# Zeroing the experts' row table ahead, in the first attention, instead of padding behind each expert's last row

## The reference, cut to what matters

```
L0 attention: h = silu(x W1' + b1) W2' + b2;  q,k,v = h Wg' + bg  (16 heads of 64)
              dots = q k' / 8, masked where j >= i + 64; softmax; @ v; @ Wo' + bo
L0 ffn:       logits = -|x - keys|^2 + x rw' + rb  over 16 experts; the best 4; w = softmax(top 4)
              expert e: gelu(x w1[e]' + b1[e]) w2[e]' + b2[e]  (512 hidden);  sum of the 4 by w
L1 attention: 16 heads of 8, LoRA of rank 16 on all four projections
L1 ffn:       a scan of gates over 16 steps of 256 rows, then tanh
```

## Time and profile before

| | |
|---|---|
| median of 3 runs | 1598.92 us (1596.56 to 1600.42) |
| the profiled execution's own time | 1603.28 us |
| its span, first to last instruction | 1601.5 us |
| mean granted TensorE clock | 0.921 of full |
| first attention | 0 to about 691 us |
| first transpose of the experts | 712.1 us |
| HBM read / written | 46.87 / 27.33 MB |

### The profile page before, as it was taken

How to read it: one execution, slowest core, us unless ns; L and a number is a source line. 1 busy time by engine, 2 the same in 40 slices (tenths; PEclk the granted TensorE clock), 3 DMA queues, 4 the chain that set the end, 5 groups by cost and what they waited for, 6 DMA issues and landing times.

```text
span 1601.5 us, 37212 instructions
## 1 busy us (share of the span) xinstructions
PE 1305.1 (81%) x9486; PEld 975.0 (61%) x9486; DVE 1059.0 (66%) x3801; ACT 960.6 (60%) x2716; POOL 785.4 (49%) x898
## 2 busy tenths in 40 slices
PE   7999999999999999746799999703778777787871
PEld 3766666666666666436799999602445445455540
DVE  1677777777777777637766666414776767777646
ACT  5877777777777777423455555302565656556654
POOL 1567777777777777624400000276656655652003
PEclk9999999999999999958999999956898989889986
DMA  9100000000000000021122222123423223232101
GB/s 343 45 8 16 13 11 13 13 13 13 13 13 13 13 13 14 16 66 55 49 66 66 66 66 66 54 50 54 81 49 77 54 51 75 46 72 43 31 0 53
DMA packets 77063, 75.02 MB, mean 47 GB/s; under 512 B 10913, under 2 KB 66977, under 8 KB 75330
## 3 DMA queue, kind: packets, MB, share of 16 engines
q1 hardware_dynamic: 67506, 56.86, 13.9%
q0 software_dynamic: 8192, 16.79, 3.8%
q10 hardware_dynamic: 1296, 0.59, 0.1%
HBM read 46.87 MB, written 27.33 MB: 46 GB/s over the span
## 4 chain that ended last, share of the span: by engine, by line
PE 32%; issue 6%; ACT 5%; DVE 5%; POOL 3%; DVEq 2%; POOLq 2%; SPq 1%; DMA 0%; ACTq 0%
PE psum L818 8%; PE psum L829 7%; PE psum L862 3%; PE psum L851 3%; PE psum L926 3%; POOL yk L567 2%; ACT qst L1098 2%; PE psum L942 2%; PE psum L943 1%; ACT wall L1054 1%; ACT wall L1098 1%; DVE wA L1292 1%; PE psum L798 1%; PE psum L884 1%; DVEq L1431 1%
## 5 line engine op out<-in xcount | busy, mean ns | idle before, releaser
L503 POOL TENSOR_SCALAR P<-P,rinv 128x192 f32<-128x192 f32 (+1 forms) x384 | 308.8, 818 | 164.4 <-DVE rinv L1170 162.7
L1010 ACT ACTIVATE P<-shifted,least 128x192 f32<-128x192 f32 (+1 forms) x512 | 240.2, 471 | 126.4 <-DVE least L1156 125.1
L1044 ACT ACTIVATE hid<-psum,wA 128x128 f32<-128x128 f32 x576 | 164.9, 369 | 146.8 <-PE psum L818 146.7
L1368 DVE TENSOR_REDUCE mx<-psum 128x2 f32<-128x512 f32 x256 | 164.4, 685 | 82.6 <-PE psum L926 79.2
L1156 DVE CUSTOM_DVE_ANT_0 shifted<-psum,band 128x192 f32<-128x192 f32 (+1 forms) x512 | 168.7, 384 | 30.5 <-PE psum L695 30.2
L1054 ACT ACTIVATE wall<-psum 128x1024 f32<-128x1024 f32 x128 | 131.2, 1025 | 83.5 <-PE psum L851 81.2
L818 PE MATMUL psum<-xgT,wA 128*128 128x128 f32 x1152 | 162.3, 285 | 18.0 <-DVE xgT L1299 16.3
L818 PEld LDWEIGHTS psum<-xgT,wA 128*128 128x128 f32 x1152 | 143.7, 196 | 25.6 <-issue 25.3
L493 POOL DMA_INDIRECT xs<-x1c,pos x128 | 128.0, 1000 | 55.9 <-issue 28.2
L829 PE MATMUL psum<-wB,hid 128*128 128x128 f32 x1152 | 154.0, 278 | 0.0
L567 POOL DMA_INDIRECT yk<-ys,posc x128 | 123.7, 967 | 49.5 <-issue 37.1
(11 more groups left out here) (247 smaller groups left out, 2671.8 us busy)
## 6 DMA issues: line engine op xcount, KB each, us to landing
xg<-xs SPq DMA_DIRECT2D x144, 64.0 KB, 1.8
ys<-yrow SPq DMA_DIRECT2D x72, 128.0 KB, 1.9
wall<-in_wall SPq DMA_DIRECT2D x1, 8232.0 KB, 36.6
qkd<-parts SPq DMA_DIRECT2D x32, 192.0 KB
qst<-qkd SPq DMA_DIRECT2D x66, 64.0 KB
wall<-qkd SPq DMA_DIRECT2D x35, 64.0 KB
kst<-qkd SPq DMA_DIRECT2D x11, 192.0 KB
hT<-in_xT SPq DMA_DIRECT2D x4, 512.0 KB, 6.1
```

The lines of the kernel that those rows point to most:

```text
L503: g.tensor_scalar(x, x, rinv[:, par, n:n + 1], None, ALU.mult).then_inc(s["pn_ready"], 1)
L1010: last = sc.activation(P[:, par, it, h, 0:w], shifted[:, par, it, h, 0:w], ACT.Exp, scale=-1.0, bias=least[:, par, n:n + 1], accum_out=row ...
L1044: sc.activation(hid[:, p, f, :], UP[two][:, at:at + GT], ACT.Gelu, bias=wA[:, p, F + f:F + f + 1]).then_inc(s["hid_ready"], 1)
L1368: v.tensor_reduce(out=mx[:, :, h], in_=SB[(par + 1 + h) % 3].rearrange("q (i n) -> q i n", i=TT), axis=mybir.AxisListType.X, op=ALU.max).t ...
```

## The change

The fill no longer depends on the counts. SyncE, once it has issued the weight loads, writes zeros over the whole table in 34 transfers: 33 of them write 128 rows of each of the 16 sections (1 MB, in pieces of 512 bytes), the last writes the 128 rows at `DUMMY` (64 KB). From the fifth on, two are let go a batch, by `wo_mm`. An even one also waits until the earlier ones have landed. GpSimd gets one more wait a batch, ahead of the first scatter: the rows that this batch can reach must be filled. All pads, their `value_load`s, three VectorE instructions (L1269 to L1271) and ScalarE's two waits go.

```
-        def pad(eng, e):
-            at = eng.value_load(pad_at[0:1, e:e + 1], min_val=0, max_val=DUMMY) if e < E else DUMMY
-            eng.dma_start(xs[bass.ds(at, GT), :], zrow[:, :]).then_inc(s["pad_in"], 16)
...
+            sp.wait_ge(s["zrow_ready"], 1)
+            rows = xs[0:DUMMY, :].rearrange("(e r) d -> r e d", e=E)
+            nothing = zrow[:, :].rearrange("q (o d) -> q o d", o=1).to_broadcast([128, E, D])
+            for c in range(CAP // 128):
+                if c % 2 == 0 and c > 0:
+                    sp.wait_ge(s["filled"], 16 * c)
+                if c >= 4:
+                    sp.wait_ge(s["wo_mm"], PAIRS * (c // 2 - 1))
+                sp.dma_start(rows[128 * c:128 * c + 128, :, :], nothing).then_inc(s["filled"], 16)
+            sp.dma_start(xs[DUMMY:ROWS, :], zrow[:, :]).then_inc(s["filled"], 16)
+
             sp.wait_ge(s["plan_ready"], 1)
             sp.dma_start(plan_d, plan2[:, :, :].rearrange("q k c -> q (k c)")).then_inc(s["plan_out"], 16)
-            sp.wait_ge(s["zrow_ready"], 1)
-            for e in range(3):
-                pad(sp, e)
             sp.wait_ge(s["plan_out"], 16)
             sp.dma_start(plan[:, :], plan_d.rearrange("(o t) c -> o (t c)", o=1)).then_inc(s["plan_in"], 16)
-            for e in range(3, E // 2):
-                pad(sp, e)
             sp.wait_ge(s["plan_in"], 16)
-            sp.wait_ge(s["pad_in"], 16 * (E + 1))
+            sp.wait_ge(s["filled"], 16 * (CAP // 128 + 1))
...
                         if p == 0:
                             need_alone(pool, "pos_ready", b - 1)
+                            need_alone(pool, "filled", 32 * (b - 1))
...
-            act.wait_ge(s["plan_ready"], 1)
-            act.wait_ge(s["zrow_ready"], 1)
-            for e in range(E // 2, E + 1):
-                pad(act, e)
...
-            v.tensor_tensor(skip[:, :], count[:, :], first_row[:, :], ALU.add)
-            v.drain()
-            v.tensor_copy(pad_at[:, :], skip[:, :])
```

More of the change, by code:

```diff
@@ L128, in build @@
         past = sb("past", [128, E])
-        skip = sb("skip", [128, E])
         ended = sb("ended", [128, 2, E])
@@ L135, in build @@
         plan2 = sb("plan2", [128, 2, 2], i32)
-        pad_at = sb("pad_at", [128, E], i32)
         plan = sb("plan", [1, 512], i32)
@@ L277, in build @@
             m_y var_ready pow_ready x1c_ready m_x x1T_ready m_l mask_ready m_r pos_ready xsq_ready x1_kept scat exp_w top_ready
-            ksq_ready rmat_ready a_done plan_ready zrow_ready plan_out plan_in pad_in
+            ksq_ready rmat_ready a_done plan_ready zrow_ready plan_out plan_in filled
             b2_mm xg_in0 xg_in1 xg_in2 xg_in3 tin_mm xgT_ready wA_ready wB_ready up_mm hid_ready dn_mm yrow_ready ys_out
```

## The result

The changed kernel is faster: 1589.93 us against 1600.29 (medians of 11 runs each), ratio 0.9948 with an interval of 0.9936 to 0.9961, about 8 us (the two medians by themselves lie 10.4 apart). Forecast were 2.3 us, 1596.6, and 1594 to 1603.

What follows compares the result with a forecast made beforehand. TensorE sets the pace, waiting at the experts' start on SyncE's pads. Removing them gives -2.4, GpSimd's wait +0.15, faster scatters -0.05, fills nothing: -2.3 us, 1598.92 to 1596.6; own range 1594.5 to 1598.5, overall 1594 to 1603.

Steps and rivals of the forecast that it cites:

- the three VectorE instructions: Plan ahead of the experts: with the drain, about 0.4 us earlier, but the plan isn't last; worth nothing.
- What bounds the kernel: TensorE sets the pace; between attention and experts it idles 15.09 us behind SyncE's queue of `value_load`s and pads.
- So the 2.4 us go through to the end.: Expert stage: one pipeline of row loads, weight copies and products, so an start 2.4 us earlier shortens the whole kernel.
- Fills: First attention: 34 fills, 34.7 MB at 287 GB/s, two in about 9 us with start and landing; cost nothing.
- rival 1: L1215: scatters queue behind fills and `x1c` stalls if under 208 GB/s; +23 us less 2.3, 1620; chance 0.08.
- Rival 2: First attention: GpSimd or another engine held beside fills, +3 to +8 us less 2.3, 1599.5 to 1604.5; chance 0.14.
- turn-taking of rings: DMA engines alternate between rings packet by packet, so a scatter keeps nearly all its 5.3 us of room before `x1c`.
- the prediction's worst case: Before `x1c`: a scatter waits for both fills, until 611.2, then needs about a microsecond; 2.7 us of room left.
- The iteration shown: Attention batch read as b = 15, with only the last two fills, let go near 602.2.
- Rival 3: Experts' start worth more: 2.95 us in place of 2.3, and a luckier clock, 1 to 2 us; 1594 to 1595.5; chance 0.12.
- The issue gap: SyncE's 0.45 us of issue at 709.43, before the first row load; may stay or go, left out of the sum.
- Rival 4: Experts' start: gain lost at once because something else holds it where it is; 1598.9 us; chance 0.02.

Runs made afterwards that it cites:

- the like pairs: Comparisons of fills against pads with VectorE's list equally long on both sides; differences -0.07%, -0.18%, -0.01%, +0.04% and +0.10%, mean -0.02%.
- the one with six more: Changed kernel with six more VectorE instructions ahead of the experts (the three removed ones, two drains, a copy); 0.9989 against the kernel before, 0.9978 to 1.0001.

## Why the prediction was wrong

The step that failed is a term that the prediction put at nothing: the three VectorE instructions "make the plan earlier; the plan isn't last, so this is worth nothing". Their own time was indeed worth nothing, 0.4 us beside a wait. But they stand ahead of everything that VectorE does later in its list. Without them the list's idle gaps fell on other instructions, and 500 us later GpSimd and VectorE met in the other order. Measured: three instructions fewer and the pads kept, 0.9957 and 0.9947, that is 7 to 8.5 us; the three kept in the changed kernel, 0.9993.

- *What bounds the kernel.* The chain through SyncE's queue, and `a_done` as what is last after it, were right; 2.26 us between last scatter and first row load against 2.3 forecast.
- *"So the 2.4 us go through to the end."* Shown up to the last transposition of the experts, where 2.2 us are left as the average of all profiles. To the end it isn't shown: the like pairs differ by 0.02% on average.
- *Fills.* 287 GB/s taken, 279 to 287 measured; about 9 us a pair; no DMA wait ahead of `x1c`. The scatters took GpSimd as long as before, but of rival 1 half came true: they did queue behind the fills, and 4.1 us in place of 1.9 to the last packet of a batch left 1.6 us of room at the least. The stall did not come, because the fills ran at 279 GB/s and more, and rival 1 needed less than 208. Rival 2 (engines held a little) asked for 3 to 8 us more; fills and pads together, 0.9997, allow about 2. The Trainium skill's turn-taking of rings (DMA: Bandwidth & Descriptors, Queues, rings and completion order), from which the prediction took that a scatter would not wait for a whole fill, is not what this trace shows. A scatter started at 360.09 sent its first packet at 364.6, after nearly 2000 packets of the fill. Why is open; the prediction's worst case, which did without turns, was the right one to keep.
- *One reading was off by an iteration.* The iteration shown is b = 14, not 15: in the kernel after, the pair let go near 602 is the last but one, and the last big fill goes at 640.3. That is still some 60 us ahead of `a_done`, and nothing else hangs on it.
- *Rival 3* had the direction but not the cause. The issue gap and a luckier clock at the experts' start were not it; the stretch of the experts took 310.3 to 312.5 us in all profiles, and went with neither.
- *Rival 4*, the gain lost at once, is not what happened at the start; in total time the like pairs can't be told from it.
- *The range* ended at 1594 and missed 1589.93, because it was built from stages that the change touches. The second attention, with ten batches between 1190 and 1450 us in which two engines start 0.1 to 0.2 us apart on the same port and each wrong order costs 1.5 us of VectorE, was not looked at. That the miss was on the fast side is luck: nothing in the prediction says which way a shorter list turns the order. The row was there to be read: 1.96 us for an operation that elsewhere in the same trace took 0.42.

Open: what makes the gaps. The Trainium skill (Runtime: NRT & Kernel Launch, Instruction fetch mechanics) says that an engine's list is loaded in blocks while it runs, and that a taken branch can interrupt this. For the branch the trace agrees. Right behind the branch at its loop's turn VectorE is idle for about 2 us, in all kernels alike; these are its idle time there in the kernel before, and the one packet in flight in 1282.2 to 1282.5, where the first of the two gaps begins:

```profile
DVE nmx L1376 <- issue: 3.9, 2, 2.1
...
q14 instruction: 1, 0.01, 11.1%
```

In all 18 profiles such a packet of 8,192 bytes starts within 0.1 us of the start of this gap. For the small gaps no load is shown, but their places are regular. Counted over all of VectorE's records in the trace, its sequencer's included, one stands at number 5855 in every kernel, and in all but the one with six more another stands at 5727, 128 earlier. So the gaps stay at their count and the list moves past them, by as many places as it was shortened. That they are the seams of the same loading is likely, and not shown.

Also open is by which steps a shifted gap changes the 0.61 us between the first gate product and GpSimd's start into 0.94. The batches mostly keep to one order, and TensorE's clock, at 1.2 GHz for 12 to 20% of this stretch, may take part in it.

## What to carry to other kernels

Where two engines contend for one port in a loop, and start within a few tenths of a microsecond of each other, fix the order by a wait; here a single wait gave 0.7 to 0.8% to the kernel before, more than the change under study. When a change removes or adds instructions early in an engine's list, test it with fillers that keep the list's length before crediting the change itself. And look in the profile for one operation of one shape with two durations.

## What the runs showed of the hardware

- Two instructions of VectorE and GpSimd on SBUF: 1.96 us for VectorE's of 0.43 when it started 0.21 us second; 2.06 for GpSimd's of 1.90 when that one was 0.12 us second.
- 1 MB of zeros from a 64 KB tile, in 512-byte pieces with rows of one partition 2 MiB + 64 KiB apart, went at 279 to 287 GB/s, beside a TensorE that was busy 38.5 us of 40 as before (300 to 340 and 580 to 620 us).
- An indirect transfer of 64 KB on another queue, started beside two such fills, sent its data only after the fill in front: last packet after 4.1 to 5.4 us, alone 1.9.
- Three instructions fewer in VectorE's list, 500 us ahead, changed the time by 0.4 to 0.5%. Three more than before changed nothing that shows (0.9989, 0.9978 to 1.0001).
- VectorE's small idle gaps stood 128 of its records apart, at the same count in every kernel. At the loop's turn it was idle for 1.8 to 2.1 us, with an 8 KB instruction packet at the gap's start.
